# The low part of the weights moves from VectorE to GpSimd, the low part of x from GpSimd to VectorE

## The reference

```
selected_W = W[cat_ids]
selected_b = b[cat_ids]
out = jnp.einsum('bsd,bdh->bsh', x, selected_W) + selected_b[:, None, :]
...
w_scale = jnp.mean(jnp.abs(weight)) + EPS
w_quant = clip(round(weight / w_scale), -1, 1)
a_scale = jnp.max(jnp.abs(x), axis=-1, keepdims=True) + EPS
a_quant = round(clip(x / a_scale * 127.0, -128.0, 127.0))
y = jnp.einsum('bsi,oi->bso', a_quant, w_quant) * (w_scale * a_scale / 127.0)
return x_in + y
```

## Time and profile before

| | us |
|---|---|
| median of 3 runs | 538.88 (538.79 to 540.0) |
| the profiled execution | 539.01 |
| its span | 537.2 |
| TensorE busy | 508.2 (95%) |
| VectorE busy | 386.9 (72%) |
| ScalarE busy | 343.2 (64%) |
| GpSimd busy | 280.2 (52%) |

### The profile page before, as it was taken

The page is one execution under the profiler, slowest core; times in us unless marked ns, Lnnn a source line. Parts: engine busy times, 40 slices in busy tenths (PEclk is TensorE's granted clock), DMA queues, the critical chain, the costliest instruction groups (busy, mean ns, idle before and its releaser), DMA issues. The chain is left out here.

```text
span 537.2 us, 13884 instructions
## 1 busy us (share of the span) xinstructions
PE 508.2 (95%) x2584; PEld 356.9 (66%) x2585; DVE 386.9 (72%) x652; ACT 343.2 (64%) x502; POOL 280.2 (52%) x396
## 2 busy tenths in 40 slices
PE   4799999999999999999999998999989999999996
PEld 1567677766776666677677675677756677777773
DVE  3686774878667867876876867867888768667754
ACT  3476665766676667756756675765857676666652
POOL 3696455445655364545556354565456555546440
PEclk9999999999999999999999999999999999999999
DMA  5799889999999999999989799988999999899943
GB/s 170 251 382 375 283 277 317 389 343 322 322 348 362 375 325 387 344 298 369 340 290 322 291 362 393 358 294 286 415 345 361 317 375 337 270 328 317 342 153 130
DMA packets 71729, 172.76 MB, mean 322 GB/s; under 512 B 8097, under 2 KB 8225, under 8 KB 64801
## 3 DMA queue, kind: packets, MB, share of 16 engines
q1 hardware_dynamic: 71712, 172.59, 90.5%
HBM read 139.00 MB, written 33.55 MB: 321 GB/s over the span
## 5 line engine op out<-in xcount | busy, mean ns | idle before, releaser
L620 PE MATMUL ps_cond<-sb_w_hi,sb_xT_hi 128*128 x512 | 221.9, 433 | 16.7 <-ACT ps_cond L346 10.7
L622 PE MATMUL ps_cond<-sb_w_hi,sb_xT_lo 128*128 x512 | 200.3, 391 | 0.0
L621 PE MATMUL ps_cond<-sb_w_lo,sb_xT_hi 128*128 x512 | 199.2, 389 | 0.0
L487 DVE TENSOR_TENSOR sb_w_lo<-sb_w_raw,sb_w_hi x106 | 156.2, 1512 | 28.8 <-issue 22.0
L317 POOL TENSOR_TENSOR sb_xT_lo<-sb_xT_raw,sb_xT_hi 128x512 fp32r<-128x512 f32 x128 | 165.5, 1293 | 10.9
L406 ACT ACTIVATE sb_a_rounded<-ps_cond,sb_rounder,sb_a_inv 128x512 f32<-128x512 f32 x128 | 99.5, 777 | 94.8 <-DVE sb_a_inv L534 91.7
L334 POOL TENSOR_SCALAR sb_y_scale<-sb_absmax,sb_w_step 128x1 f32<-128x1 f32 x128 | 40.9, 320 | 219.1 <-DVE sb_absmax L528 208.7
L528 DVE TENSOR_REDUCE sb_absmax<-ps_cond 128x1 f32<-128x512 f32 x128 | 87.9, 686 | 93.1 <-PE ps_cond L622 81.9
L620 PEld LDWEIGHTS ps_cond<-sb_w_hi,sb_xT_hi 128*128 128x128 f32 x512 | 96.3, 188 | 57.9 <-issue 31.4
L588 PE MATMUL ps_y<-sb_ffnT,sb_aT 128*128 128x512 bf16 x512 | 131.5, 379 | 1.7 <-ACT sb_aT L396 1.6
L355 ACT ACTIVATE sb_w_hi<-sb_w_raw x106 | 106.4, 1052 | 20.6 <-issue 11.2
(11 more groups left out here) (69 smaller groups left out, 35.0 us busy)
## 6 DMA issues: line engine op xcount, KB each, us to landing
sb_w_raw<-cond_w SPq DMA_DIRECT2D x53, 1024.0 KB, 6.6
sb_xT_raw<-x_t SPq DMA_DIRECT2D x128, 256.0 KB, 5.1
sb_x_rows<-x SPq DMA_DIRECT2D x128, 256.0 KB, 5.1
out<-sb_x_rows SPq DMA_DIRECT2D x128, 256.0 KB, 4.8
sb_bias<-cond_b SPq DMA_DIRECT2D x54, 256.0 KB, 7.6
sb_ffn_raw<-ffn_t SPq DMA_DIRECT2D x1, 1024.0 KB, 6.9
sb_w_raw<-cond_w SPq DMA_DIRECT2D x4, 256.0 KB, 7.2
sb_cat_row_i<-itok SPq DMA_DIRECT2D x1, 64.0 KB, 3.6
```

The costliest lines, as they stand in the source:

```text
L487: dve.tensor_tensor(w_lo[:, bass.ds(at, PIECE)], w_raw[:, bass.ds(at, PIECE)], w_hi[:, bass.ds(at, PIECE)].bitcast(F32), ALU.subtract).the ...
L620: pe.matmul(ps_cond, x_hi_k, w_hi_k, start=False, stop=False, skip_group_check=True)
L621: pe.matmul(ps_cond, x_hi_k, w_lo_k, start=False, stop=False, skip_group_check=True)
L622: last_mm = pe.matmul(ps_cond, x_lo_k, w_hi_k, start=False, stop=(k == KD - 1), skip_group_check=True)
```

## The change

`split_low` for the weights moves from VectorE to GpSimd, with its table load and its branch; it stands there behind `y_scale`. Of x, GpSimd keeps the high part (`x_high`), and VectorE makes the low part (`x_low`), between the reciprocal and the result of three steps back, and waits there for `x_hi_done`. VectorE no longer reads the table. How far ahead each part is made stays as it was: three steps for the low part of the weights, two for both parts of x. The four pieces of the very first weight (L479) stay on VectorE, with the low part of x of step 0 ahead of them.

```diff
--- before.py
+++ after.py
@@ -308,24 +308,40 @@
             pool.affine_select(out=ident[:, :], in_=ident[:, :], compare_op=ALU.is_equal, fill=0.0,
                                base=0, pattern=[[-1, P]], channel_multiplier=1).then_inc(consts_done, 1)
 
-            def split_x(step, n):
+            def x_high(step, n):
                 m = n % XT_RING
                 pool.wait_ge(xT_loaded[m], xT_landed(step, m))
                 pool.sem_inc(x_taken, 1)
                 pool.tensor_copy(xT_hi[:, m, :], xT_raw[:, m, :]).then_inc(x_hi_done, 1)
-                pool.wait_ge(x_hi_done, step + 1)
-                pool.tensor_tensor(xT_lo[:, m, :], xT_raw[:, m, :], xT_hi[:, m, :].bitcast(F32),
-                                   ALU.subtract).then_inc(x_lo_done, 1)
+
+            def split_low(new, offset, step):
+                with pool.If(new > 0):
+                    for piece in range(PIECES):
+                        at = offset + piece * PIECE
+                        pool.wait_ge(w_hi_done, (step - 1) * PIECES + piece + 1)
+                        pool.tensor_tensor(w_lo[:, bass.ds(at, PIECE)], w_raw[:, bass.ds(at, PIECE)],
+                                           w_hi[:, bass.ds(at, PIECE)].bitcast(F32), ALU.subtract).then_inc(w_lo_done, 1)
+                with pool.Else():
+
+                    if type(step) is not int or step > 1:
+                        pool.wait_ge(w_lo_done, (step - 1) * PIECES)
+                    pool.sem_inc(w_lo_done, PIECES)
 
             for step in range(X_AHEAD):
-                split_x(step, step)
+                x_high(step, step)
+            pool.wait_ge(table_done, 1)
+            for step in range(1, LO_AHEAD):
+                new, offset = w_slot(pool, step)
+                split_low(new, offset, step)
 
             def body(r0, u, first, last):
                 r = r0 + u
+                if not last or u + LO_AHEAD < U:
+                    new, offset = w_slot(pool, r + LO_AHEAD)
                 if not last or u + X_AHEAD < U:
                     if not first or u + X_AHEAD >= XT_RING:
                         pool.wait_ge(cond_mm_done, r + X_AHEAD - XT_RING + 1)
-                    split_x(r + X_AHEAD, (u + X_AHEAD) % U)
+                    x_high(r + X_AHEAD, (u + X_AHEAD) % U)
                 s = u % STAT_RING
                 if first and u == 0:
                     pool.wait_ge(ffn_scaled, 1)
@@ -333,6 +349,8 @@
                 pool.sem_inc(absmax_taken, 1)
                 pool.tensor_scalar(y_scale[:, s:s + 1], absmax[:, s:s + 1], EPS, w_step[:, 0:1],
                                    ALU.add, ALU.mult).then_inc(y_scale_done, 1)
+                if not last or u + LO_AHEAD < U:
+                    split_low(new, offset, r + LO_AHEAD)
 
             over_steps(pool, body)
 
@@ -474,28 +492,22 @@
             dve.tensor_copy(table[:, 0:B, 0:CAT_COLUMNS],
                             cond_ps[COND_BANKS - 1][0:1, :].rearrange("a (b c) -> a b c", c=CAT_COLUMNS)).then_inc(table_done, 1)
 
+            dve.wait_ge(x_hi_done, 1)
+            dve.tensor_tensor(xT_lo[:, 0, :], xT_raw[:, 0, :], xT_hi[:, 0, :].bitcast(F32),
+                              ALU.subtract).then_inc(x_lo_done, 1)
             for k in range(KD):
                 dve.wait_ge(w0_hi_done, k + 1)
                 dve.tensor_tensor(w_lo[:, k * H:(k + 1) * H], w_raw[:, k * H:(k + 1) * H],
                                   w_hi[:, k * H:(k + 1) * H].bitcast(F32), ALU.subtract).then_inc(w0_lo_done, 1)
 
-            def split_low(new, offset, step):
-                with dve.If(new > 0):
-                    for piece in range(PIECES):
-                        at = offset + piece * PIECE
-                        dve.wait_ge(w_hi_done, (step - 1) * PIECES + piece + 1)
-                        dve.tensor_tensor(w_lo[:, bass.ds(at, PIECE)], w_raw[:, bass.ds(at, PIECE)],
-                                          w_hi[:, bass.ds(at, PIECE)].bitcast(F32), ALU.subtract).then_inc(w_lo_done, 1)
-                with dve.Else():
-
-                    if type(step) is not int or step > 1:
-                        dve.wait_ge(w_lo_done, (step - 1) * PIECES)
-                    dve.sem_inc(w_lo_done, PIECES)
-
-            dve.wait_ge(table_done, 1)
-            for step in range(1, LO_AHEAD):
-                new, offset = w_slot(dve, step)
-                split_low(new, offset, step)
+            def x_low(step, n):
+                m = n % XT_RING
+                dve.wait_ge(x_hi_done, step + 1)
+                dve.tensor_tensor(xT_lo[:, m, :], xT_raw[:, m, :], xT_hi[:, m, :].bitcast(F32),
+                                  ALU.subtract).then_inc(x_lo_done, 1)
+
+            for step in range(1, X_AHEAD):
+                x_low(step, step)
 
             def ternary_begin():
                 dve.wait_ge(ffn_sum_mm_done, 1)
@@ -532,15 +544,14 @@
                                   ALU.add, ALU.mult).then_inc(a_step_done, 1)
                 dve.wait_ge(a_step_done, r + 1)
                 dve.reciprocal(a_inv[:, s:s + 1], a_step[:, s:s + 1]).then_inc(a_inv_done, 1)
+                if not last or u + X_AHEAD < U:
+                    x_low(r + X_AHEAD, (u + X_AHEAD) % U)
                 if first and u == 0:
                     ternary_begin()
                 elif first and u == 1:
                     ternary_end()
                 elif not first or u >= Y_BEHIND:
                     result(r - Y_BEHIND, (u - Y_BEHIND) % U)
-                if not last or u + LO_AHEAD < U:
-                    new, offset = w_slot(dve, r + LO_AHEAD)
-                    split_low(new, offset, r + LO_AHEAD)
 
             over_steps(dve, body)
             for u in range(U - Y_BEHIND, U):
```

## The result

| | before | after |
|---|---|---|
| median, us | 538.84 (537.9 to 540.0, 4 runs) | 558.12 (556.69 to 564.4, 4 runs) |
| the profiled execution's span, us | 537.2 | 555.0 |
| ratio | | 1.0379, 95% interval 1.0294 to 1.0464 |

The change made the kernel slower, by 19.3 us where 32.6 were forecast. The forecast stood at 571.6 with a range from 556 to 600, so the way was forecast rightly and the size too large.

What follows compares the result with a forecast made beforehand. TensorE's 3.85 us beat was the bound, with 19.9 us lost to other engines. GpSimd's longer steps would lose 48.5 instead, +28.6, plus 4 for late weights: 539.0 + 32.6 = 571.6 us, range 556 to 600.

Steps and rivals of the forecast that it cites:

- The bound and the rule: TensorE's 3.85 us step is the beat; closely following new categories overrun it, summed over their distances less spare: 48.5 us lost.
- the 0.2 us of spare: Kernel before, VectorE: spare at the head of each chain, taken off 22.8 us to give the 19.9 lost.
- Distance 2: New categories two steps apart, 16 places: GpSimd's 6.27 + 2.2 against 7.70 us, 12.3 us lost.
- GpSimd's step: GpSimd's step with a new category: y_scale 0.27, x_low 0.69, two pieces 4.70, x_high 0.61, together 6.27 us.
- The spare of a lone category: TensorE's wait for x_low: a lone new category leaves 0.43 us, 0.35 after semaphores, taken off 14 times, 4.9 us.
- 14 chains: Runs of new categories one or two steps apart, cut wherever a longer distance stands; each has spare once, at its head.
- Late weights: Weight slots freed later by GpSimd, so loads arrive later: 4 us added, with 0 and 8 as ends.
- the main case: Shared SBUF access: GpSimd and VectorE alternate by whole instruction, x_low going between y_scale and the first piece; used in the sum.
- the kept way: Rival at the shared SBUF access: GpSimd holds it through y_scale and both pieces, x_low waits 4.70 more; 597 us, chance 0.16.
- Dear pieces: Rival: a GpSimd piece of the weights' low part takes 2.58 us, making its step 6.73; 590 us, chance 0.13.
- Not slower: Rival: GpSimd's piece is short enough, deciding at 2.05 us; 532 us at 1.97; chance 0.05, shared with idle time covering all.
- idle time on GpSimd would cover it: Rival: GpSimd's 48% idle absorbs the pieces, 539 us; chance 0.05, shared with the short piece.

Runs made afterwards that it cites:

- a quarter of x_low: Kernel after, with x_low made for only the first 128 of 512 columns, the rest zero: 534.34 us, ratio 0.9928.
- the short pieces: Kernel after, with 896 instead of 1024 columns in each GpSimd piece of the weights' low part: 536.02 us, ratio 0.9943.
- weights only: Kernel before, with the weights' low part moved to GpSimd, which also keeps both parts of x: 599.16 us, ratio 1.1143.
- y_scale on VectorE: Kernel after, with y_scale made by VectorE behind the reciprocal instead of by GpSimd: 557.04 us, ratio 1.0345 to the kernel before.
- x_high alone three ahead: Kernel after, with GpSimd's x_high made three steps ahead and VectorE's x_low left at two: 541.06 us, ratio 1.0046.
- x only: Kernel before, with x_low moved to VectorE, which keeps the weights' low part; GpSimd makes x_high and y_scale: 528.25 us, ratio 0.9805.
- x only with early load: Kernel before, with x_low moved to VectorE and VectorE's table load ahead of its wait for the first product: 523.28 us, ratio 0.9707.

## Why the prediction was too high

**The bound and the rule: right.** The time is set by how often new categories follow each other closely, not by shares. That the rule gave the 19.9 us of before was no test, since the 0.2 us of spare was chosen so that it did; no row shows it. But put with the measured terms, the rule gives the measured time after. The 17 neighbouring x_high stood 5.92 to 6.03 us apart, 5.96 in the mean: 17 x (5.96 - 3.85) = 35.9. Distance 2 measured 8.18 over both steps, 16 x (8.18 - 7.70) = 7.7. Less 14 x 0.58 = 8.1, this makes 35.5 us lost. Measured are 37.9, of which up to 3.1 are the clock, below. The rule also foretold a quarter of x_low and the short pieces (16 and 15 against 14.1 and 15.3); for weights only it was 20 us too high (95 against 75.2).

**GpSimd's step: the term that was too large.** The prediction put y_scale 0.27 and x_low 0.69 one behind the other, 6.27 in all. The trace has 5.96: y_scale stands still while x_low runs and ends with it. This counts 0.31 in the 17 distances of one and 0.29 in the 16 of two, 9.9 us, and again in the spare. The piece itself was right (2.35 said, 2.40 measured, back to back 2.36), and so was the step without a category (2.2 said, 8.18 - 5.96 = 2.22 measured).

**The spare of a lone category** was put at 0.35 and measured at 0.58. On 14 chains this is 3.2 us; it is y_scale once more, which I had counted ahead of x_low. Both terms together are the 13 us between 48.5 and 35.5.

**Late weights: 4 us that did not come.** ScalarE did wait longer for what comes with the weights:

```profile
ACT sb_w_hi L373 <- DMA sb_bias<-cond_b: 37.0, 33, 1.9
```

37.0 us against 7.8 before. But in TensorE's waits neither GpSimd's pieces nor a transfer has a row; ScalarE is four steps ahead and takes it up. These 4 us nearly cancel against the 3 of the clock, which the prediction did not have; that is luck.

**The shared access: the main case held in the kernel after.** The 127 x_low of the kernel after took 0.67 to 0.76 each, so none of them stood behind a piece:

```profile
L506 DVE TENSOR_TENSOR sb_xT_lo<-sb_xT_raw,sb_xT_hi x127: 672/693/756, 18.8 to 539.4; 128x512 fp32r<-128x512 f32 x127
```

The longest step was 6.06 us, not the 8 of the kept way. y_scale on VectorE showed how near the other case was: with the piece 0.07 us ahead, x_low waited for the first piece, but not for the second. The rule of the Trainium skill ("SBUF — State Buffer", section "SBUF: two separate sides") is that whoever starts first holds the shared ports for its whole instruction; this 2.84 us agrees with one instruction and not two. But it does not always stay at one. With x_high alone three ahead, GpSimd's and VectorE's timelines have:

```profile
398.43 4.72 POOL L323 TENSOR_TENSOR sb_w_lo<-sb_w_raw,sb_w_hi  x2
403.10 0.61 POOL L316 CAST sb_xT_hi<-sb_xT_raw 128x512 fp32r<-128x512 f32 x1
403.69 0.69 POOL L351 TENSOR_SCALAR sb_y_scale<-sb_absmax,sb_w_step 128x1 f32<-128x1 f32 x1
```

```profile
399.20 5.05 DVE L507 TENSOR_TENSOR sb_xT_lo<-sb_xT_raw,sb_xT_hi 128x512 fp32r<-128x512 f32 x1
```

This x_low asked at 399.20 while the first piece ran, and was over at 404.25, behind both pieces and the x_high after them: the kept way of the rival, once, where the other 45 long ones of that run took at most 2.95. What decides between the two was not found.

**The rivals.** Dear pieces (2.58) is refuted by 2.40. The Trainium skill's "GPSIMD Engine Reference", section 3.1, gives about 2.6 cycles for an element with two inputs; at 1.2 GHz that is an estimate of 2.17 ns a column, so 2.22 us for 1024 columns. The prediction's 2.5 us is that only with y_scale's 0.26 put on top, and the measured piece lies between the two. As a slope the trace agrees with the page: from 1.289 us at 512 columns to 2.400 at 1024 are 2.17 ns a column, and the short piece of 896 columns, 2.123 us, lies on the same line. What stands in front of it is then 0.18 us, by the same rows. My line through y_scale, at 2.0 ns a column, was too flat. Not slower: the short pieces show that this was a real way, with the point near 2.18 us and not at 2.05. That idle time on GpSimd would cover it is refuted by the kernel after itself, with 28% of it idle.

**Half of the change was good.** Taken apart, x_low on VectorE is worth -10.6 us and the weights on GpSimd alone +60. The prediction looked at the change only as a whole, where the second half made GpSimd's list the limit and the first half took 0.82 us a step from it (6.83 in weights only, 6.01 in both).

## What to carry to other kernels

Where work comes in bursts, count the bursts and compare the engine's step with the beat in them; here the mean share gave no hint. What stands behind a long piece of work on an in-order engine inherits its time: moving the small instruction that others wait for ahead of it (x_high three ahead) gave back 17 us without making any work cheaper. A change made of two moves is worth pricing move by move, since one of them may be the gain.

## What the runs showed of the hardware

**TensorE's clock fell behind long waits.** At full speed the products of a step start 0.23 us apart. Step 52 of the kernel after began when TensorE had stood still for 1.95 us. Its timeline:

```profile
234.66 0.49 PE L631 MATMUL ps_cond<-sb_w_hi,sb_xT_hi 128*128 x1 [1.95 <-DVE sb_xT_lo L506]
...
235.92 0.56 PE L633 MATMUL ps_cond<-sb_w_hi,sb_xT_lo 128*128 x1
236.28 0.63 PE L631 MATMUL ps_cond<-sb_w_hi,sb_xT_hi 128*128 x1
236.71 0.63 PE L632 MATMUL ps_cond<-sb_w_lo,sb_xT_hi 128*128 x1
237.13 0.63 PE L633 MATMUL ps_cond<-sb_w_hi,sb_xT_lo 128*128 x1
```

From 236.28 on they start 0.43 apart. The granted clock of the stretch before and of this one, by windows (us, busy time of each engine, then the clock):

```profile
228.60:234.66 6.06, 4.11 (x20) 2.71 (x21) 2.33 (x6) 1.87 (x3) 5.94 (x5) 1.00 0.85 317
234.66:238.80 4.14, 4.14 (x12) 2.97 (x12) 2.63 (x6) 2.44 (x4) 1.10 (x3) 0.66 0.64 236
```

0.66 over the stretch is the upper level (2.4 GHz) for a part and the lower (1.2 GHz) for the rest. This happened at steps 52 and 79, each 5.36 us long instead of 3.78, so up to 3.1 us of the time are the clock's. Weights only, where TensorE stood still up to 2.7 us, has seven such stretches, and y_scale on VectorE in the kernel after has three; the kernel before, x only and x only with early load have none. The length of one wait does not decide it alone: step 43 waited 1.91 us, shown above, and kept its clock, and in the kernel before with x three ahead one step lost it behind two shorter waits, 1.53 and 0.52 us. The four runs of the kernel after have mean clocks of 0.992, 0.998, 0.981 and 0.989 and times of 556.7, 556.7, 564.4 and 559.5. The two with the lowest clocks are the slowest, but the first two took the same time at different clocks, so the clock doesn't account for all of it. A wait on TensorE can thus cost more than its length, and no term of the prediction had this. What exactly makes the clock fall was not tried.

**Order of asking decides at the shared access.** An x_low of VectorE, with two inputs in SBUF, that asks 0.07 us behind a GpSimd piece waits for nearly all of it, 2.15 us; one that asks before the piece costs GpSimd its own 0.69. Once, in x_high alone three ahead, an x_low that asked in the middle of a piece waited 4.36 us, until three instructions of GpSimd were over.
